# Second attention: the accumulated outputs copied out of PSUM by VectorE, not by ScalarE

## The chip, the cores and the metric

The kernel runs on one core of a Trainium2 chip: TensorE (PE) multiplies matrices into PSUM, ScalarE (ACT) and VectorE (DVE) work on PSUM and SBUF, GpSimd (POOL) on SBUF, and SyncE (SP) issues DMAs. Each engine takes its instructions in order, and engines wait for one another on semaphores. The metric is the device time of one execution in microseconds, lower is better.

## What is computed

Four sublayers follow each other on x of shape (8, 512, 128), each with a residual and a layer norm: an attention with softmax, a mixture of experts, a second attention with sigmoid weights, and a gated feed-forward. The change lies in the third. From the reference:

```python
def _L1_attn_ref(x, q_w, q_b, k_w, k_b, v_w, v_b, o_w, o_b, qn_scale, kn_scale):
    q = rms_norm(x, qn_scale) @ q_w.T + q_b
    k = rms_norm(x, kn_scale) @ k_w.T + k_b
    v = x @ v_w.T + v_b                      # 16 heads of 8
...
    q = apply_rotary(q, cos, sin)
    k = apply_rotary(k, cos, sin)
    scores = jnp.einsum('bhqd,bhkd->bhqk', q, k) * scale
    weights = jax.nn.sigmoid(scores)
    weights = weights / (jnp.sum(weights, axis=-1, keepdims=True) + EPS_RENORM)
    attn = jnp.einsum('bhqk,bhkd->bhqd', weights, v)
    attn = attn.transpose(0, 2, 1, 3).reshape(B, L, D)
    return attn @ o_w.T + o_b
...
x = _layernorm(x + _L1_attn_ref(x, ...))
```

## The kernel before

The second attention (`attention1`, from L1195) works batch by batch, 8 in all, b = 0 to 7. A batch is 32 steps, u = 0 to 31, and each engine has its own function `units` that says what it does at each step. The function `walk` (L270) calls it: batch 0 up to step 16, then a hardware loop over three pairs of batches, then the last one and a half batches unrolled. The order on each engine is thus fixed by the code, and the engines are held together by semaphores only.

At each step TensorE computes the scores of two heads against 128 keys (`s2`, L1321, into `ps_s[:, u % 2]`, two buffers), and ScalarE takes their sigmoid over 128x1024 elements into `prob` (L1275). Scores of step u wait for sigmoid u-2. At each odd step TensorE multiplies the probabilities of the two steps before with V (`pv`, L1333): product e stands at step 2e + 3, and sixteen of them make a batch. Eight products, for eight heads, accumulate in one PSUM bank, `ps_o`; then it must be copied to SBUF (`osb[:, n]`) before the next eight begin, since there is only one such bank. This copy is `take_o` (L1265), on ScalarE at the steps with u % 16 == 1, behind the sigmoid of that step: at step 17 for the first half of a batch (n = 0), at step 1 of the next batch for the second half (n = 1), and once after the last step. It counts up `o_taken`. Two users wait for that: product 8 (or 0 of the next batch) at step 19 or 3, and `turn_o` at step 20 or 4, where TensorE transposes `osb` into `ps_t`. The value also carries the sum of the weights, by which VectorE then divides (`divide`, L1463).

Other work is spread over the steps (constants at L66 to L71). For the finished batch, steps 4 to 15 hold the transposes, the projection with o_w, the residual and the norm. For a batch two ahead, VectorE starts `rms` at step 16 (L1415: copy of x, square, sum, scale; the four lines L1420 to L1427), POOL takes the power (L1548), VectorE multiplies x by it at step 19 (`scale_x`, L1431), and at steps 18, 20, 24 and 28 TensorE and VectorE do `front_use` and `take_front`: transposes of x and of the scaled x, and projections with rotary factors. V of the next batch is computed at step 2 (L1293) and taken by VectorE (L1458). The work for the batch two ahead exists for b = 0 to 5, V of the next batch in the loop for b = 1 to 6 at step 2. In the last batch VectorE also prepares feed-forward weights from step 18.

`osb` has two halves and is overwritten only after the transposes of one batch before (the wait on `ot_done`). After the block, `LastOutput` (L1577) goes on with the last half inside the feed-forward.

Of the kernel before, what the change touches and what calls it, by code (L numbers as in the profile page):

```python
# [12 lines left out]
ACT = mybir.ActivationFunctionType  # L13
# [3 lines left out]
NB = 8  # L17
T = 512
NT = T // P
# [5 lines left out]
PER_O = 2  # L25
NO = NG // PER_O
# [10 lines left out]
NE = NG * NT  # L37
# [84 lines left out]
def is_first(b):  # L122

    return isinstance(b, int) and b == 0


def is_last(b):

    return isinstance(b, int) and b == NB - 1
# [54 lines left out]
def v_tiles(flat):  # L184

    return flat[:, SLOT:].rearrange("p (k h c) -> p k h c", k=NT, h=H)
# [8 lines left out]
def output_parts(ps):  # L195

    return ps.rearrange("p (k j q c) -> p k j q c", k=NT, j=HG, q=PER_O)
# [8 lines left out]
def divide_outputs(nc, att, n, o, rec, done):  # L206

    to, spread = outputs_of(att, n), [P, NT, HG, HD]
    for q in range(PER_O):
        ins = nc.vector.tensor_tensor(to[:, :, :, q, :], o[:, :, :, q, 0:HD],  # L210
                                      rec[:, :, :, q].unsqueeze(3).broadcast_to(spread), ALU.mult)
    ins.then_inc(done, 1)
# [57 lines left out]
def walk(eng, units, loop_u=LOOP_U, lead=True):  # L270

    if lead:
        units(-1, 1, 0, NU, True, True, False, False)
    units(0, 0, 0, loop_u, False, True, True, False)
    with eng.Fori(0, (NB - 2) // 2) as i:
        for q in range(2):
            units(2 * i + q, q, loop_u, NU, True, True, True, False)
            units(2 * i + q + 1, 1 - q, 0, loop_u, False, True, True, True)  # L280
    units(NB - 2, 0, loop_u, NU, False, True, True, False)
    units(NB - 1, 1, 0, loop_u, False, False, True, True)
    units(NB - 1, 1, loop_u, NU, False, False, True, False)
# [911 lines left out]
def attention1(ctx, nc, g, c, e, xh, xl, ff):  # L1195
# [3 lines left out]
    with ExitStack() as inner:  # L1199
        def sb(name, shape, dt=F32):  # L1200
            return ctx.enter_context(nc.sbuf_tensor("a1_" + name, shape, dt))

        def sem(name):
            return ctx.enter_context(nc.semaphore("a1_" + name))
# [11 lines left out]
        osb = sb("osb", [P, 2, T])  # L1216
# [5 lines left out]
        ps_o = inner.enter_context(nc.psum_tensor("a1_ps_o", [P, T], F32))  # L1222
# [8 lines left out]
        s2_done, exp_done, pv_done = sem("s2_done"), sem("exp_done"), sem("pv_done")  # L1231
        o_taken, ot_done, rec_done, att_done, sum_done = (
            sem(n) for n in ("o_taken", "ot_done", "rec_done", "att_done", "sum_done"))


        S2_C, EXP_C, PV_C, O_C, OT_C, ATT_C = NU, 2, PSLOTS // 2, 1, 2, 1
# [4 lines left out]
        @block.sync  # L1241
        def _(sp):
            def step(b, p, qk_on, front):
                if front:

                    sp.wait_ge(s2_done, NU * b + S2_C)
                    load_stacks(sp, e, (qs[1 - p], ks[1 - p]), b + 1, 1 - p)
                if qk_on:
                    parts_to_dram(sp, e, b + 2, p)

            for src, ints, _, _ in ff["weights"]:
                sp.dma_start(ints[:, :, :], src).then_inc(ff["in"], 16)
            parts_to_dram(sp, e, 1, 1)
            with sp.Fori(0, (NB - 2) // 2) as i:
                step(2 * i, 0, True, True)
                step(2 * i + 1, 1, True, True)
            step(NB - 2, 0, False, True)

        @block.scalar
        def _(act):  # L1260
            def take(dst, src, ready, value, done):
                act.wait_ge(ready, value)
                nc.scalar.activation(dst, src, ACT.Copy).then_inc(done, 1)

            def take_o(b, n):  # L1265
                act.wait_ge(ot_done, NO * b + n - 1 + OT_C)
                take(osb[:, n, :], ps_o[:, :], pv_done, NE * b + PER_O * NT * (n + 1) + PV_C, o_taken)

            def units(b, p, u0, u1, qk_on, front, back, tail):
                for u in range(u0, u1):  # L1270
                    if back:
                        act.wait_ge(s2_done, NU * b + u + 1 + S2_C)
                        if u % 2 == 0:
                            act.wait_ge(pv_done, NE * b + u // 2 - PSLOTS // 2 + 1 + PV_C)
                        nc.scalar.activation(prob[:, u % PSLOTS, :, :], ps_s[:, u % 2, :, :], ACT.Sigmoid,  # L1275
                                             scale=float(HD) ** -0.5).then_inc(exp_done, 1)
                    if u % 16 == 1 and (back if u > 16 else tail):
                        take_o(*((b, u // 16 - 1) if u > 16 else (b - 1, NO - 1)))

            act.sem_inc(exp_done, EXP_C)  # L1280
            act.sem_inc(o_taken, O_C)
            walk(act, units, LOOP_U1, False)
            take_o(NB - 1, NO - 1)

        @block.tensor
        def _(pe):
# [122 lines left out]
        def _(dve):  # L1409
# [41 lines left out]
            def take_v(b, p):  # L1451

                if not isinstance(b, int) or b >= 2:
                    dve.wait_ge(pv_done, NE * (b - 1) + PV_C)
                if isinstance(b, int) and b < 2:
                    dve.wait_ge(cleared, 2 * b + 2)
                dve.wait_ge(v_done, b + 1)
                nc.vector.tensor_tensor(v_tiles(va[p])[:, :, :, 0:HD],  # L1458
                                        ps_f[:, 1, :].rearrange("p (k h d) -> p k h d", k=NT, h=H),
                                        vb[:, :].rearrange("p (h d) -> p h d", h=H).unsqueeze(1).broadcast_to(  # L1460
                                            [P, NT, H, HD]), ALU.add).then_inc(v_taken, 1)

            def divide(b, n):  # L1463

                o = output_parts(ps_t[:, :, :].rearrange("p k d -> p (k d)"))
                dve.wait_ge(ot_done, NO * b + n + 1 + OT_C)
                nc.vector.tensor_scalar_add(rec[:, :, :, :], o[:, :, :, :, HD], RENORM_EPS).then_inc(rec_done, 1)
                dve.wait_ge(rec_done, 2 * (NO * b + n) + 1)
                nc.vector.reciprocal(rec[:, :, :, :], rec[:, :, :, :]).then_inc(rec_done, 1)
                dve.wait_ge(rec_done, 2 * (NO * b + n) + 2)  # L1470
                divide_outputs(nc, att, n, o, rec, att_done)
# [30 lines left out]
            def units(b, p, u0, u1, qk_on, front, back, tail):  # L1502
                for u in range(u0, u1):
                    if is_first(b) and u == 0:
                        rms(1)
                    if is_first(b) and u == FIRST_AT[0] - 1:
                        scale_x(1)
                    if is_first(b) and u in FIRST_AT:
                        take_front(1, 1, FIRST_AT.index(u))
                    if front and u == (V_FIRST_AT if is_first(b) else V1_AT):  # L1510
                        take_v(b + 1, 1 - p)
                    if u % 16 == TURN_AT and (back if u > 16 else tail):
                        divide(*((b, u // 16 - 1) if u > 16 else (b - 1, NO - 1)))
                    if back and is_last(b) and u in FFN_W_AT:
                        if u == FFN_W_AT[0]:
                            dve.wait_ge(ff["in"], 16 * len(ff["weights"]))
                            dve.wait_ge(rope_done, 2 * NB + R_C)
                        prepare_ffn_weights(nc, dve, ff, turned[:, 0, 0:HID].rearrange("p (n d) -> p n d", n=NH3),
                                            u - FFN_W_AT[0])
                    if u == ALL_AT and tail:  # L1520
                        take_all(b - 1)
                    if u == PROJECT_AT and tail:
                        add_x(b - 1)
                    if u == NORM1_AT and tail:
                        norm(b - 1)
                    if u == X_AT and tail:
                        part_x(b - 1)
                    if u == RMS_AT and qk_on:
                        rms(b + 2)
                    if u == SCALE_AT and qk_on:  # L1530
                        scale_x(b + 2)
                    if u in FRONT_AT and qk_on:
                        take_front(b + 2, p, FRONT_AT.index(u))

            layernorm_stats(nc, dve, e["ln"], NB - 1, e["y"])
            take_v(0, 0)
            walk(dve, units, LOOP_U1, False)

        @block.gpsimd
        def _(pool):  # L1540
# [935 lines left out]
```

## Time and profile before

| | us |
|---|---|
| median of 3 runs | 1075.75 |
| lowest, highest | 1074.6, 1077.48 |
| the profiled execution | 1074.96 |
| its span, first to last instruction | 1073.2 |
| TensorE busy in the span | 1003.9 (94%) |
| VectorE | 814.2 (76%) |
| ScalarE | 735.5 (69%) |
| POOL | 459.8 (43%) |

The second attention's steps lie between about 722 and 1007 us of the span. Busy shares are of the whole span and mix stages with different limits; the table says little about this one. TensorE's rows come twice, PE for the matrix products and PEld for the loading of weights, which overlaps them; an idle time and its releaser stand in the row of the instruction that waited. Rows of one activation may overlap the next by their ends.

### The profile page before, as it was taken

To read this page: it belongs to the slowest core of one execution; us is meant where nothing else is said; L and a number is where in the kernel's file an instruction comes from. 1 tells how busy PE (TensorE), PEld (TensorE's weight loads), DVE (VectorE), ACT (ScalarE), POOL (GpSimd) and SP (SyncE) were. 2 spreads that over 40 slices of the span, in tenths; PEclk is the share of its full clock that TensorE was granted. 3 is DMA by queue.
4 is the path that set the end of the run, shared out by engine and by line. 5 is a ranking of instruction groups with operands and counts; after the bars stand their busy time and mean duration, and the time that the engine had idled before them with its cause. 6 is when DMAs were issued, how large, how long until landed. Compare 5 with 4: busy or idle time off the path is not lost. (4 is left out here: it accounts for less than half of the span.)

```text
span 1073.2 us, 20047 instructions
## 1 busy us (share of the span) xinstructions
PE 1003.9 (94%) x5764; PEld 473.8 (44%) x5764; DVE 814.2 (76%) x1891; ACT 735.5 (69%) x952; POOL 459.8 (43%) x464
## 2 busy tenths in 40 slices
PE   3999999999999998999999999989999999999996
PEld 1122222222222234788888887763332323222485
DVE  4879999999999975987888789957456545632577
ACT  1057777777777776555555555557888898899754
POOL 0313314133142715676777677565331333220175
PEclk7579999999999999999999999999999999999999
DMA  7363122231222003244323422441512331230011
GB/s 194 111 213 106 55 76 85 70 104 55 75 85 60 2 2 105 94 123 141 113 93 130 139 103 87 139 149 62 167 56 74 117 111 58 66 117 2 1 30 49
DMA packets 74091, 97.00 MB, mean 90 GB/s; under 512 B 12716, under 2 KB 42284, under 8 KB 73644
## 3 DMA queue, kind: packets, MB, share of 16 engines
q1 hardware_dynamic: 73048, 95.17, 28.5%
q10 hardware_dynamic: 992, 1.21, 0.4%
q8 instruction: 25, 0.41, 0.2%
q14 instruction: 26, 0.21, 0.1%
HBM read 68.16 MB, written 27.79 MB: 89 GB/s over the span
## 5 line engine op out<-in xcount | busy, mean ns | idle before, releaser
L688 DVE TENSOR_REDUCE a_nmax<-a_ps_f 128x1 f32<-128x512 f32 x512 | 320.1, 684 | 27.4 <-PE a_ps_f L543 26.3
L471 ACT ACTIVATE a_prob<-a_ps_s 128x1024 f32<-128x1024 f32 x256 | 251.2, 1022 | 74.8 <-PE a_ps_s L608 73.5
L1275 ACT ACTIVATE a_prob<-a_ps_s 128x1024 f32<-128x1024 f32 x256 | 244.9, 1030 | 35.6 <-PE a_ps_s L1329 34.8
L2102 POOL TENSOR_TENSOR moe_hl<-moe_hid,moe_hh 128x512 fp32r<-128x512 f32 x135 | 175.5, 1305 | 90.0 <-ACT moe_hh L1987 89.9
L543 PE MATMUL a_ps_f<-a_ks,a_qs 48*128 48x512 bf16 x512 | 176.9, 414 | 24.1 <-DMA a_ks<-parts_k 10.4
L1977 ACT ACTIVATE moe_ps<-moe_ps 128x512 f32<-128x512 f32 x128 | 74.5, 582 | 112.1 <-PE moe_ps L1904 111.5
L621 PE MATMUL a_ps_o<-a_prob,a_va 128*32 128x512 f32 x1024 | 138.1, 612 | 0.5 <-ACT a_prob L471 0.4
L1342 PE MATMUL a_ps_o<-a_prob,a_va 128*32 128x512 f32 x1024 | 137.2, 608 | 1.0 <-ACT a_prob L1275 0.5
L543 PEld LDWEIGHTS a_ps_f<-a_ks,a_qs 48*128 48x128 bf16 x512 | 40.7, 94 | 218.9 <-DVE a_nmax L688 188.3
L608 PE MATMUL a_ps_s<-a_qs,a_ks 51*128 51x512 bf16 x512 | 135.0, 388 | 1.7 <-ACT a_prob L471 1.5
L2028 DVE TENSOR_TENSOR moe_prod<-moe_cw,moe_ps 128x512 f32<-128x512 f32 x128 | 87.4, 683 | 29.3 <-PE moe_ps L1904 28.6
L1329 PE MATMUL a_ps_s<-a_qs,a_ks 48*128 48x512 bf16 x512 | 92.8, 388 | 12.3 <-ACT a_prob L1275 8.9
L2037 DVE TENSOR_TENSOR moe_hid<-moe_prod,moe_ps 128x512 f32<-128x512 f32 x128 | 87.0, 680 | 6.9 <-DVE moe_prod L2028 1.9
L259 POOL TENSOR_TENSOR a_parts<-a_qk,g_zero 128x512 bf16<-128x512 f32 x28 | 29.3, 1046 | 138.1 <-ACT a_qk L443 66.1
L1987 ACT ACTIVATE moe_hh<-moe_hid 128x512 fp32r<-128x512 f32 x136 | 84.6, 623 | 3.9 <-DVE moe_hid L2037 3.7
L1329 PEld LDWEIGHTS a_ps_s<-a_qs,a_ks 48*128 48x128 bf16 x512 | 23.6, 93 | 132.9 <-ACT a_prob L1275 106.0
L750 POOL TENSOR_TENSOR a_msplit<-a_nmax,g_zero 128x32 bf16<-128x32 f32 x16 | 3.8, 240 | 146.5 <-DVE a_nmax L688 146.5
L1902 PE MATMUL moe_ps<-moe_xh,moe_whig 128*128 (+1 forms) x136 | 54.8, 403 | 2.1 <-DVE moe_hid L2037 2.1
L1927 PE MATMUL moe_ps<-moe_hl,moe_whid 128*128 128x512 f32 x136 | 53.9, 396 | 1.4 <-POOL moe_hl L2102 1.4
L1902 PE MATMUL moe_ps<-moe_xh,moe_whiu 128*128 (+1 forms) x136 | 53.8, 395 | 0.0
L1922 PE MATMUL moe_ps<-moe_hh,moe_wlod 128*128 128x512 f32 x136 | 53.8, 395 | 0.0
L1903 PE MATMUL moe_ps<-moe_xh,moe_wlog 128*128 (+1 forms) x136 | 53.6, 394 | 0.0
(297 smaller groups left out, 1588.0 us busy)
## 6 DMA issues: line engine op xcount, KB each, us to landing
moe_cw<-r_weights SPq DMA_DIRECT2D x256, 128.0 KB, 2.9
parts_q<-a_parts SPq DMA_DIRECT2D x48, 256.0 KB, 2.5
a_qs<-parts_q SPq DMA_DIRECT2D x128, 96.0 KB, 2.4
parts_k<-a_parts SPq DMA_DIRECT2D x46, 256.0 KB, 2.5
a_ks<-parts_k SPq DMA_DIRECT2D x121, 96.0 KB, 2.4
a_xt<-in_x_t SPq DMA_DIRECT2D x8, 256.0 KB, 2.9
out_x<-g_X SPq DMA_DIRECT2D x7, 256.0 KB, 2.3
moe_wg<-in_wg SPq DMA_DIRECT2D x1, 1088.0 KB, 6.7
```

What stands on the lines that cost most here:

```text
L471: nc.scalar.activation(prob[:, u % PSLOTS, :, :], ps_s[:, u % 2, :, :], ACT.Exp, scale=float(P) ** -0.5).then_inc(exp_done, 1)
L543: nc.tensor.matmul(ps_f[:, bank, :], stack_rows(qs[p], h, QKR)[:, qt * P:(qt + 1) * P], stack_rows(ks[p], h, QKR), start=True, stop=True). ...
L608: mm = nc.tensor.matmul(ps_s[:, u % 2, i, :], stack_rows(ks[p], h, MXR)[:, kt * P:(kt + 1) * P], stack_rows(qs[p], h, MXR), start=True, st ...
L621: mm = nc.tensor.matmul(ps_o[j * CT:(j + 1) * CT, :], v_of_head(va[p], kt, grp * HG + j), prob[:, (2 * e + j // UN) % PSLOTS, j % UN, :], ...
L688: nc.vector.tensor_reduce(nmax[:, half_no, h % 2, col:col + 1], ps_f[:, bank, :], AX.X, ALU.max, negate=True).then_inc(max_done, 1)
L1275: nc.scalar.activation(prob[:, u % PSLOTS, :, :], ps_s[:, u % 2, :, :], ACT.Sigmoid, scale=float(HD) ** -0.5).then_inc(exp_done, 1)
L1329: mm = nc.tensor.matmul(ps_s[:, u % 2, i, :], stack_rows(ks[p], h, QKR)[:, kt * P:(kt + 1) * P], stack_rows(qs[p], h, QKR), start=True, st ...
L1342: mm = nc.tensor.matmul(ps_o[j * CT:(j + 1) * CT, :], v_of_head(va[p], kt, grp * HG + j), prob[:, (2 * e + j // UN) % PSLOTS, j % UN, :], ...
L1902: nc.tensor.matmul(dst, w[0][:, j, :], hi, start=True, stop=False)
L2028: nc.vector.tensor_tensor(prod[:, bank(j), :], cw[:, slot(j), :], ps_u[:, bank(j), :], ALU.mult).then_inc(prod_done, 1)
L2037: nc.vector.tensor_tensor(hid[:, hid_at(j), :], prod[:, bank(j), :], ps_g[:, bank(j), :], ALU.mult).then_inc(hid_done, 1)
L2102: nc.gpsimd.tensor_tensor(hl[:, part_at(j), :], hid[:, hid_at(j), :], hh[:, part_at(j), :], ALU.subtract).then_inc(hl_done, 1)
```

## The change

`take_o` goes from ScalarE's program to VectorE's. It stands there at the same steps, u % 16 == 1, ahead of `divide` and behind `take_v`, with the same waits and the same semaphore, as a `tensor_copy` in place of an activation with the function Copy. The last copy follows VectorE's walk. Nothing else is changed.

```diff
         @block.scalar
         def _(act):
-            def take(dst, src, ready, value, done):
-                act.wait_ge(ready, value)
-                nc.scalar.activation(dst, src, ACT.Copy).then_inc(done, 1)
-
-            def take_o(b, n):
-                act.wait_ge(ot_done, NO * b + n - 1 + OT_C)
-                take(osb[:, n, :], ps_o[:, :], pv_done, NE * b + PER_O * NT * (n + 1) + PV_C, o_taken)
-
             def units(b, p, u0, u1, qk_on, front, back, tail):
...
-                    if u % 16 == 1 and (back if u > 16 else tail):
-                        take_o(*((b, u // 16 - 1) if u > 16 else (b - 1, NO - 1)))
...
             walk(act, units, LOOP_U1, False)
-            take_o(NB - 1, NO - 1)
...
+            def take_o(b, n):
+                dve.wait_ge(ot_done, NO * b + n - 1 + OT_C)
+                dve.wait_ge(pv_done, NE * b + PER_O * NT * (n + 1) + PV_C)
+                nc.vector.tensor_copy(osb[:, n, :], ps_o[:, :]).then_inc(o_taken, 1)
+
             def divide(b, n):
...
                     if front and u == (V_FIRST_AT if is_first(b) else V1_AT):
                         take_v(b + 1, 1 - p)
+                    if u % 16 == 1 and (back if u > 16 else tail):
+                        take_o(*((b, u // 16 - 1) if u > 16 else (b - 1, NO - 1)))
                     if u % 16 == TURN_AT and (back if u > 16 else tail):
                         divide(*((b, u // 16 - 1) if u > 16 else (b - 1, NO - 1)))
...
             walk(dve, units, LOOP_U1, False)
+            take_o(NB - 1, NO - 1)
```

The place at step 17 on VectorE, in the loop. The names are those of the code (`a_` for the tiles of the attentions); REGISTER_ALU and ISA rows compute or wait for the value of a semaphore. Before:

```order
L1425 TENSOR_REDUCE a_ms<-a_xr 128x4 [waits a1_x_step]
L1426 REGISTER_ALU
L1427 TENSOR_SCALAR a_ms<-a_ms 128x4 [waits a1_x_step]
L1437 COPY a_xt<-a_ps_f 128x512 [waits a1_f_done]
L1430 REGISTER_ALU
L1431 TENSOR_TENSOR a_xr<-a_xb,a_rr 128x512 [waits a1_x_pow]
```

And now (lines of VectorE's program are 11 smaller up to `take_o`, since eight lines of ScalarE's are gone and three elsewhere):

```order
L1414 TENSOR_REDUCE a_ms<-a_xr 128x4 [waits a1_x_step]
L1415 REGISTER_ALU
L1416 TENSOR_SCALAR a_ms<-a_ms 128x4 [waits a1_x_step]
L1453 ISA
L1454 REGISTER_ALU [waits a1_ot_done]
L1455 COPY a_osb<-a_ps_o 128x512 [waits a1_pv_done]
L1426 COPY a_xt<-a_ps_f 128x512 [waits a1_f_done]
L1419 REGISTER_ALU
L1420 TENSOR_TENSOR a_xr<-a_xb,a_rr 128x512 [waits a1_x_pow]
```

The copy of `ps_o` stands between the last instruction of `rms` and the copy of the transposed x, with two more instructions on registers ahead of it, and the scaling of x (x_pow) is behind it.

The same place on ScalarE before:

```order
L1272 REGISTER_ALU
L1275 ACTIVATE a_prob<-a_ps_s 128x1024 [waits a1_s2_done]
L1266 ISA
L1262 REGISTER_ALU [waits a1_ot_done]
L1263 ACTIVATE a_osb<-a_ps_o 128x512 [waits a1_pv_done]
L1272 REGISTER_ALU
L1275 ACTIVATE a_prob<-a_ps_s 128x1024 [waits a1_pv_done,a1_s2_done]
```

And now:

```order
L1267 ACTIVATE a_prob<-a_ps_s 128x1024 [waits a1_s2_done]
L1264 REGISTER_ALU
L1266 REGISTER_ALU [waits a1_s2_done]
L1267 ACTIVATE a_prob<-a_ps_s 128x1024 [waits a1_pv_done]
L1264 REGISTER_ALU
```

The row of the copy and the two ahead of it are gone, and sigmoid follows sigmoid.

## Rows read from the trace of the kernel before

**Rows 1.** Stretch; busy of PE, PEld, DVE, ACT, POOL; TensorE clock; DMA share, GB/s

```profile
742.00:1006.00 264.00, 247.78 (x1752) 76.84 (x1744) 131.57 (x322) 236.05 (x256) 74.54 (x73) 1.00 0.27 84
```

**Rows 2.** Groups of instructions, 715 to 1010 us: busy us, mean ns | idle before

```profile
L1275 ACT ACTIVATE a_prob<-a_ps_s 128x1024 f32<-128x1024 f32 x256 | 244.9, 1030 | 35.6 <-PE a_ps_s L1329 34.8
...
L1342 PEld LDWEIGHTS a_ps_o<-a_prob,a_va 128*32 128x32 f32 x1024 | 20.2, 108 | 34.7 <-issue 28.5 <-ACT a_prob L1275 3.0 <-ACT a_osb L1263 2.3
```

**Rows 3.** The same view: copies out of PSUM on ScalarE and VectorE

```profile
L1263 ACT ACTIVATE a_osb<-a_ps_o 128x512 f32<-128x512 f32 x16 | 9.8, 612 | 1.2 <-PE a_ps_o L1342 1.2
...
L1475 DVE COPY a_att_t<-a_ps_t 128x512 f32<-128x512 f32 x7 | 4.8, 692 | 7.9 <-PE a_ps_t L1362 7.9
```

**Rows 4.** Timeline, place A: start us, us, engine, line, operation [idle <-releaser]

```profile
781.59 0.60 ACT L1263 ACTIVATE a_osb<-a_ps_o 128x512 f32<-128x512 f32 x1
...
782.06 0.69 DVE L1425 TENSOR_REDUCE a_ms<-a_xr 128x4 f32<-128x512 f32 x1
...
782.07 2.88 ACT L1275 ACTIVATE a_prob<-a_ps_s 128x1024 f32<-128x1024 f32 x3
...
782.26 0.16 PEld L1342 LDWEIGHTS a_ps_o<-a_prob,a_va 128*32 128x32 f32 x8 [0.23 <-ACT a_osb L1263]
...
782.78 0.17 DVE L1427 TENSOR_SCALAR a_ms<-a_ms 128x4 f32<-128x4 f32 x1
...
782.86 0.68 DVE L1437 COPY a_xt<-a_ps_f 128x512 f32<-128x512 f32 x1
...
783.26 0.10 PEld L1329 LDWEIGHTS a_ps_s<-a_qs,a_ks 48*128 48x128 bf16 x2 [0.84 <-ACT a_prob L1275]
...
783.58 0.42 PEld L1355 LDWEIGHTS a_ps_t<-g_ident,a_osb 128*128 128x128 f32 x4 [0.23 <-issue]
...
784.07 0.69 DVE L1431 TENSOR_TENSOR a_xr<-a_xb,a_rr 128x512 f32<-128x512 f32 x1 [0.53 <-POOL a_rr L1548]
...
784.81 0.42 PEld L1312 LDWEIGHTS a_ps_f<-g_ident,a_xr 128*128 128x128 f32 x4 [0.82 <-DVE a_xr L1431]
...
785.40 0.10 PEld L1329 LDWEIGHTS a_ps_s<-a_qs,a_ks 48*128 48x128 bf16 x2 [0.17 <-issue]
...
785.84 1.02 ACT L1275 ACTIVATE a_prob<-a_ps_s 128x1024 f32<-128x1024 f32 x1 [0.89 <-PE a_ps_s L1329]
...
924.25 0.60 ACT L1263 ACTIVATE a_osb<-a_ps_o 128x512 f32<-128x512 f32 x1
```

**Rows 5.** Timeline, VectorE, a waiting register instruction between two operations

```profile
771.80 0.69 DVE L1479 TENSOR_TENSOR a_att<-a_ps_t,a_ob 128x512 f32<-128x512 f32 x1 [2.04 <-PE a_ps_t L1369]
...
772.63 0.69 DVE L1482 TENSOR_TENSOR a_att<-a_att,g_X 128x512 f32<-128x512 f32 x1
```

**Rows 6.** Timeline, place B, start of batch 2

```profile
799.11 0.63 ACT L1263 ACTIVATE a_osb<-a_ps_o 128x512 f32<-128x512 f32 x1
...
800.05 0.69 DVE L1458 TENSOR_TENSOR a_va<-a_ps_f,a_vb 128x512 f32<-128x512 f32 x1 [2.86 <-PE a_ps_f L1295]
...
800.39 3.77 ACT L1275 ACTIVATE a_prob<-a_ps_s 128x1024 f32<-128x1024 f32 x4 [0.65 <-PE a_ps_s L1329]
...
800.41 0.16 PEld L1342 LDWEIGHTS a_ps_o<-a_prob,a_va 128*32 128x32 f32 x8 [0.42 <-issue]
```

**Rows 7.** Timeline, place A of batch 0, and place D

```profile
749.16 0.42 PEld L1312 LDWEIGHTS a_ps_f<-g_ident,a_xr 128*128 128x128 f32 x4 [1.77 <-DVE a_xr L1431]
...
1007.57 0.60 ACT L1263 ACTIVATE a_osb<-a_ps_o 128x512 f32<-128x512 f32 x1 [1.25 <-PE a_ps_o L1342]
```

**Rows 8.** Timeline, place C, step 17 of batch 7

```profile
991.17 0.69 DVE L1500 TENSOR_TENSOR ff_xl<-a_ps_t,ff_xh 128x512 fp32r<-128x512 f32 x1
...
992.76 0.10 PEld L1329 LDWEIGHTS a_ps_s<-a_qs,a_ks 48*128 48x128 bf16 x2 [0.80 <-ACT a_prob L1275]
...
993.25 0.16 PEld L1342 LDWEIGHTS a_ps_o<-a_prob,a_va 128*32 128x32 f32 x8 [0.39 <-ACT a_osb L1263]
...
995.26 0.19 DVE L1467 TENSOR_SCALAR a_rec<-a_ps_t 128x32 f32<-128x32 f32 x1 [2.74 <-PE a_ps_t L1355]
```

## The prediction, made before the result was known

> **What bounds the kernel now.** The stretch to read is the second attention. The row that groups it [rows 1] shows TensorE busy 247.78 of 264 us, ScalarE 236.05, VectorE 131.57, at a granted clock of 1.00 (2.4 GHz). So TensorE and ScalarE are both nearly full, and VectorE is half empty. That share doesn't say which of the two full engines a shorter ScalarE queue would help; the gaps do. The groups of instructions [rows 2] give the two sides of one chain: the sigmoids (L1275, 256 of them) wait 34.8 us for scores from TensorE, and the products with V (L1342) wait 2.3 us for the ScalarE copy. ScalarE alternates with TensorE: scores have two buffers, so a score step u waits for the sigmoid of u-2 and the sigmoid of u for the scores of u. Where ScalarE runs without a gap, it sets the pace; where TensorE also has projections or transposes to do, TensorE does. Next the prices of the copy [rows 3], then each kind of place where one stands, in the timeline [rows 4 to 8].
>
> **Sixteen places, four kinds.** A copy stands behind step 1 and step 17 of each batch, and one after the last step. By the timeline they are: A, step 17 of batches 0 to 5, where VectorE has the RMS work of a later batch queued ahead of it (6 places, of which batch 0 is special); B, step 1 of batches 1 to 6, where TensorE computes V of the next batch (6); C, step 17 of batch 6 and steps 1 and 17 of batch 7, with none of that (3); D, the last one (1).
>
> **Place A, batches 1 to 5 (five places, from 781.59 to 924.25, so 35.67 us apart, one batch).** Before, the ScalarE copy starts at 781.59 and the next sigmoid at 782.07, so the copy takes 0.48 us of ScalarE's queue; its row says 0.60 because ends overlap. It ends at 782.19 and TensorE's first V product of the new group starts at 782.26, 0.07 later [rows 4]. That product can't start earlier than o_taken. Afterwards the copy is VectorE's, in order behind L1427, which starts at 782.78 because it ends the chain copy, square, sum, scale of the RMS work. The next VectorE instruction starts at 782.86 today, with no register instruction between; the new copy has two ahead of it, one with a wait (the order above shows them). What these cost isn't shown in isolation. The nearest rows: L1482 follows L1479 by 0.83, or 0.14 after its end, with one such waiting instruction between [rows 5], whereas L1427 follows the end of L1425 by 0.03 [rows 4]. So one costs about 0.10; from below nothing, if they are fetched while L1427 runs; from above 0.18 for two. A gain is excluded, since they stand ahead of the copy. I take 0.09: copy from 782.95, and 0.69 long, by L1475, the same form out of PSUM on VectorE [rows 3]. It ends at 783.64, and the product starts at 783.71 instead of 782.26, 1.45 later.
>
> Not all of this reaches the end. Behind the product stand scores 20 (1.00 later, by 782.26 to 783.26), the transposes of the output (0.32 more), then transposes of the scaled input, which today stand idle until 784.81, "0.82 <-DVE a_xr", then scores 21 at 785.40, 0.59 further [rows 4]. With the late product these come at 784.71, 785.03, 785.62 (transposes of this form take 0.59) and 786.21. Is the scaled input ready at 785.62? VectorE now runs copy until 783.64, L1437 (0.68) until 784.35, and L1431 (0.69) until 785.07, as POOL's power is ready by 784.07: yes, with 0.5 to spare. So the late product costs 786.21 - 785.40 = 0.81 us; 0.64 of its 1.45 is swallowed by a wait that existed. ScalarE's sigmoid after scores 21 starts 0.44 behind them, with an idle gap of 0.89 ahead of it [rows 4]: it waits for TensorE, so the 0.48 us that the removed copy frees only makes that gap longer. Sigmoid 21 and all behind it start 0.81 later. Register instructions at nothing or 0.18 give 0.72 to 0.90. From there both engines run in lockstep, POOL and DMA work hangs on the same steps, and I find no wait later in the batch for something that didn't move. Five times: +4.05 us.
>
> **Place A, batch 0.** There TensorE stands at the scaled input until 749.16, for 1.77 us [rows 7]. That wait is behind the V product and longer than the 1.45 us by which the product could be late, so it hides all of it: 0, and 0.1 if it leaks.
>
> **Place B.** The copy on ScalarE starts at 799.11, yet ScalarE then still idles 0.65 us, until 800.39, for scores that TensorE starts only after V [rows 6]. Without the copy that gap grows to 1.1 us and nothing starts earlier. VectorE is idle for 2.86 us before L1458 at 800.05 [rows 6]; a 0.69 us copy there is over by about 799.7, ahead of the V product at 800.41 that needs it. Six times 0; from above 0.1 each if POOL's work beside it slows the copy.
>
> **Place C.** Here the copy delays something: the V product at 993.25 stands 0.39 "<-ACT a_osb", whereas scores 19 were issued at 992.76, and 0.32 behind them it could go, at 993.08 [rows 8]. VectorE finished its transposed input at 991.86 and has only weight preparation for much later; its copy ends near 992.7. So TensorE goes 0.17 earlier. ScalarE's sigmoids start 0.48 earlier at first, but the one that needs scores 22 comes 0.17 earlier only. Three times -0.17: -0.51 us. The weight work is pushed 0.7 us, under VectorE's later idle time of 2.74 us [rows 8].
>
> **Place D.** The last V product ends, ScalarE copies from 1007.57 and the next part of the program begins behind that [rows 7]. VectorE, idle there, takes 0.69 for 0.61 [rows 3]: +0.08 us.
>
> **A rule against the change.** The copy rows say 691 ns on VectorE against 612 on ScalarE [rows 3], 0.08 us. By the Trainium skill, "Advanced Engine Details and Errata", The Read-Write Bubble, "ScalarE is closer to PSUM, VectorE is closer to SBUF - use accordingly". Rule and rows agree on the sign, but duration alone would make at most 16 times 0.08, 1.3 us; what the queue ahead of the copy adds is not in that rule, and it is the larger part here.
>
> **Sum.** +4.05 + 0 + 0 - 0.51 + 0.08 = +3.6 us. The profiled execution took 1074.96 us (1.76 more than its span, and 0.8 under the median of 1075.75), so 1078.6 on its own scale and 1079.4 on the median's. With the register cost at either end, +3.2 to +4.1.
>
> **Rivals.** First, faster, because ScalarE is the bound. 16 times 0.48 is 7.7 us, which gives 1068.1. For it: ScalarE is at 236 of 264 us and VectorE at 132 [rows 1]. Against: in A and B ScalarE is idle right behind the copy [rows 4, 6]. [...] 0.08.
>
> Second, no measurable change: the 0.81 is made good later in each batch. It decides if behind scores 21 TensorE has slack against ScalarE again before ScalarE's lateness counts, as ScalarE has had its copy taken out. For: TensorE waits for sigmoids often in the stretch. Against: sigmoid 21 itself waits for scores. Then only -0.51 + 0.08 is left, about 1075.3. 0.15.
>
> Third, slower by more: the cover under the late product is gone. The 0.64 counted as hidden rests on the scaled input being ready at 785.62. If L1437 and L1431, pushed behind the new copy, finish over 0.55 later than I reckon (by POOL's port traffic or register instructions), the input is itself late. Then the whole 1.45 goes through: 5 x 1.45 = 7.25, less 0.43, about 1082.5. For: VectorE is in order and takes two 128x512 operations ahead of L1431. Against: the 0.5 of room. 0.10.
>
> **Numbers.** Forecast 0.67, rivals 0.08, 0.15 and 0.10. About 0.3% (3.2 us) is what a measurement can tell from no change, and the line is at 1079.0, near my forecast: I give three quarters of the forecast's chance to slower and one quarter to no change. Slower: 0.50 + 0.10 = 0.60. No change: 0.17 + 0.13 = 0.30. Faster: 0.10, with a little from the second rival. The forecast's own range is 1078.5 to 1080.5. The range reaches over rivals two and three, 1074.8 to 1082.6, and leaves out the first.
>
> **What would show each step.** In the profile of after: at place A the copy on VectorE right behind the scale instruction of the RMS work, TensorE idle some 1.4 us for it ("<-DVE a_osb"), and the wait for a_xr gone or small; the batch period 36.5 in place of 35.67 us in the loop. At B no idle time on the copy, and 1.1 us of ScalarE idle behind it. At C the product 0.2 us earlier. Wrong would be: a period of 35.67 or less, or a wait for a_xr that persists next to that for a_osb.

## The result, and the profile after

| | before | after |
|---|---|---|
| median of 5 runs | 1077.34 us | 1083.57 us |
| lowest, highest | 1074.6, 1079.11 | 1082.69, 1086.66 |
| ratio, 95% interval | | 1.0065 [1.0047, 1.0084] |
| profiled execution | 1074.96 | 1086.66 |
| its second attention, from the sigmoid of step 12 of batch 0 to the last one, start to start | 267.1 | 274.7 |

The change makes the kernel 6.2 us slower. The forecast had the side right, +3.6 us, and the size wrong by a factor of 1.7. The time lies 1.0 us above the range of 1074.8 to 1082.6. Part of that is not the change: the range was built on a median before of 1075.75 us (3 runs), which is 1077.34 with 5. As a difference, +6.2 us would still be inside the range, far from the forecast. In a second measurement (c1_changed, below) the ratio was 1.0045 [1.0024, 1.0066].

The profiled execution after is the slowest of its five, and 4.1 us of its 11.7 lie ahead of the second attention, whose first sigmoid starts at 726.9 and not at 722.8. The program up to there is the same in both kernels, and in the other profiles below this start lies anywhere between 721.9 and 725.6. So I compare stretches of the second attention, not whole spans. They begin at step 12 of batch 0, because TensorE also idles for 1.7 us where this attention begins, and around there the granted clock falls in 11 of the 14 profiles and stays at 1.00 in three; that moves the first steps by up to 1.1 us whatever the kernel. The row of the kernel before has a mean of 0.79 there:

```profile
716.00:732.00 16.00, 12.52 (x64) 5.48 (x67) 7.94 (x19) 8.07 (x10) 9.22 (x13) 0.79 0.12 37
```

Place A first, in the timeline of the kernel after, batch 1; it answers to [rows 4]. Columns: start us, us, engine, line, operation, idle before and releaser. VectorE's copy is now L1455, the V product L1331, the sigmoid L1267, the scaled input L1420.

```profile
788.21 0.17 DVE L1416 TENSOR_SCALAR a_ms<-a_ms 128x4 f32<-128x4 f32 x1
788.41 0.69 DVE L1455 COPY a_osb<-a_ps_o 128x512 f32<-128x512 f32 x1
...
789.15 0.16 PEld L1331 LDWEIGHTS a_ps_o<-a_prob,a_va 128*32 128x32 f32 x8 [1.69 <-DVE a_osb L1455]
...
789.61 0.68 DVE L1420 TENSOR_TENSOR a_xr<-a_xb,a_rr 128x512 f32<-128x512 f32 x1
790.15 0.10 PEld L1318 LDWEIGHTS a_ps_s<-a_qs,a_ks 48*128 48x128 bf16 x2 [0.84 <-issue]
...
790.47 0.42 PEld L1344 LDWEIGHTS a_ps_t<-g_ident,a_osb 128*128 128x128 f32 x4 [0.23 <-issue]
...
790.86 0.47 PEld L1301 LDWEIGHTS a_ps_f<-g_ident,a_xr 128*128 128x128 f32 x4
...
791.49 0.10 PEld L1318 LDWEIGHTS a_ps_s<-a_qs,a_ks 48*128 48x128 bf16 x2 [0.17 <-issue]
```

The copy starts 0.20 us behind the start of the last RMS instruction, and TensorE stands until it is done before it can begin the product (1.69 us in the row of the weight load, 1.40 in that of the product itself). The wait for the scaled input, 0.82 us in [rows 4], is gone: its row has no idle time. That is the chain of the forecast, step for step.

Now the same line in the five batches. These are all the copies at step 17 of batches 1 to 5, from VectorE's timeline.

```profile
788.41 0.69 DVE L1455 COPY a_osb<-a_ps_o 128x512 f32<-128x512 f32 x1
...
824.78 0.69 DVE L1455 COPY a_osb<-a_ps_o 128x512 f32<-128x512 f32 x1
...
862.69 0.69 DVE L1455 COPY a_osb<-a_ps_o 128x512 f32<-128x512 f32 x1
...
900.58 0.69 DVE L1455 COPY a_osb<-a_ps_o 128x512 f32<-128x512 f32 x1
...
936.91 0.69 DVE L1455 COPY a_osb<-a_ps_o 128x512 f32<-128x512 f32 x1
```

The batches take 36.37, 37.91, 37.89 and 36.33 us; before, all took 35.65 to 35.68. So there are two lengths: some 0.67 more than before, and 1.57 on top of that in some. Where the 1.57 lies is seen at batch 2, in the stretches of 2 us around its copy (busy time and count of PE, PEld, DVE, ACT, POOL; then the granted TensorE clock, DMA share, GB/s):

```profile
822.00:824.00 2.00, 1.85 (x16) 0.61 (x8) 1.91 (x4) 2.00 (x3) 0.00 (x0) 1.00 0.07 27
824.00:826.00 2.00, 0.59 (x6) 0.16 (x8) 1.93 (x5) 1.29 (x2) 1.01 (x1) 0.97 0.00 0
826.00:828.00 2.00, 2.00 (x12) 0.49 (x5) 0.67 (x2) 0.19 (x1) 0.00 (x0) 0.50 0.00 0
828.00:830.00 2.00, 2.00 (x14) 1.44 (x16) 1.16 (x5) 0.96 (x2) 0.00 (x0) 0.67 0.00 0
830.00:832.00 2.00, 2.00 (x20) 0.35 (x12) 1.17 (x2) 1.63 (x2) 0.00 (x0) 1.00 0.00 0
```

and in the timeline there:

```profile
825.52 1.63 PE L1331 MATMUL a_ps_o<-a_prob,a_va 128*32 128x512 f32 x8 [1.41 <-DVE a_osb L1455]
...
827.08 0.61 PE L1318 MATMUL a_ps_s<-a_qs,a_ks 48*128 48x512 bf16 x2
```

TensorE idles 1.41 us for the copy, and then its granted clock is at 0.50, 1.2 in place of 2.4 GHz, for about 3.4 us by the three rows. The eight parts of the product take 1.63 us, against 1.06 in batch 1. The row of the whole stretch before, [rows 1], has the clock at 1.00 throughout. In the execution after it falls three times between 742 and 1010 us: near 754 (batch 0), 826 and 864, each time directly behind a place where TensorE idled for 1.4 us.

### The profile page after: what moved, and what is told of

Its sections match the earlier page's. It is cut to its first block and busy times, and to the rows that moved or that the text cites. A ratio compares the mean times of both kernels' runs of the same rounds, so it can differ in the third digit from the quotient of the medians.

```text
span 1084.8 us, 20041 instructions
## 1 busy us (share of the span) xinstructions
PE 1009.2 (93%) x5764; PEld 477.3 (44%) x5764; DVE 824.9 (76%) x1907; ACT 729.9 (67%) x936; POOL 459.6 (42%) x464
## 5 line engine op out<-in xcount | busy, mean ns | idle before, releaser
L1267 ACT ACTIVATE a_prob<-a_ps_s 128x1024 f32<-128x1024 f32 x256 | 245.2, 1029 | 48.7 <-PE a_ps_s L1318 48.0
L543 PE MATMUL a_ps_f<-a_ks,a_qs 48*128 48x512 bf16 x512 | 176.4, 413 | 23.8 <-DMA a_ks<-parts_k 10.1
L1331 PE MATMUL a_ps_o<-a_prob,a_va 128*32 128x512 f32 x1024 | 139.1, 616 | 7.8 <-DVE a_osb L1455 7.2
```

The lines of the kernel that those rows point to most:

```text
L543: nc.tensor.matmul(ps_f[:, bank, :], stack_rows(qs[p], h, QKR)[:, qt * P:(qt + 1) * P], stack_rows(ks[p], h, QKR), start=True, stop=True). ...
L1331: mm = nc.tensor.matmul(ps_o[j * CT:(j + 1) * CT, :], v_of_head(va[p], kt, grp * HG + j), prob[:, (2 * e + j // UN) % PSLOTS, j % UN, :], ...
```

## The experiments

Each kernel but c2_changed and c3_filled, which have one profiled run each, was timed beside the kernel before on the same chip. The column "batch" is the distance between scaled inputs (L1431 before) of batches 1 to 5 without a fall of the clock; "stretch" goes from the sigmoid of step 12 of batch 0 to the last one; "falls" are those of the granted clock in that stretch. Batch, stretch and falls are of the one profiled run.

| kernel | median us (before) | ratio, 95% | batch us | stretch us | falls |
|---|---|---|---|---|---|
| before | | | 35.66 | 267.1 | 0 |
| after | 1083.57 (1077.34) | 1.0065 [1.0047, 1.0084] | 36.34 | 274.7 | 3 |
| c1_changed, the same | 1082.81 (1078.07) | 1.0045 [1.0024, 1.0066] | 36.34 | 273.2 | 2 |
| c2_changed, the same | 1078.86, one run | | 36.33 | 270.0 | 0 |
| e1_second_half | 1077.37 (1077.44) | 1.0004 [0.9987, 1.0021] | 35.66 | 267.0 | 0 |
| e2_first_half | 1082.65 (1077.44) | 1.0062 [1.0042, 1.0082] | 36.33 | 271.6 | 1 |
| e3_filled | 1079.6 (1077.44) | 1.0017 [0.9997, 1.0037] | 36.33 | 270.0 | 0 |
| c3_filled, the same | 1077.96, one run | | 36.33 | 270.0 | 0 |
| e4_inside_rms | 1080.48 (1077.44) | 1.003 [1.001, 1.005] | 36.14 | 270.7 | 1 |
| e5_before_late_front | 1066.01 (1076.43) | 0.9911 [0.9886, 0.9936] | 34.37 | 258.3 | 0 |
| e6_after_late_front | 1076.08 (1076.43) | 1.001 [0.9991, 1.0029] | 35.83 | 265.4 | 0 |
| e7_inside_late_front | 1067.83 (1076.43) | 0.9927 [0.9901, 0.9952] | 34.37 | 258.1 | 0 |
| e8_inside_front21 | 1078.47 (1076.43) | 1.0015 [0.9997, 1.0034] | 36.19 | 269.3 | 0 |
| c4_before_front21 | 1079.75 (1078.07) | 1.0017 [1.0006, 1.0027] | 36.19 | 269.6 | 0 |

### Which copies cost: e1_second_half and e2_first_half

e1 leaves the copies at step 17 on ScalarE and moves the others; e2 is the reverse. VectorE's side of e1:

```diff
-                    if u % 16 == 1 and (back if u > 16 else tail):
+                    if u == 1 and tail:
                         take_o(*((b, u // 16 - 1) if u > 16 else (b - 1, NO - 1)))
```

> One part of the change alone: VectorE takes only the copies at step 1 and the last one (places B, one of the three places C, and D), ScalarE keeps those at step 17. Theory: all of the loss comes from step 17 of batches 0 to 5, where the VectorE copy stands behind the RMS work. Then this kernel is as fast as before: 0 for B, -0.17 for step 1 of batch 7, +0.1 for the last, so within 1 us of before, and no wait of TensorE of over 0.5 us for the copy. Rival (each VectorE copy costs its longer duration or disturbs POOL): 8 of 16 copies moved, so about half of the loss, +3 us.

> The other part alone: VectorE takes only the copies at step 17 (places A and two of C), ScalarE keeps those at step 1. Theory: the whole loss is here. 5 x 0.69 for the late product, 2 x -0.17, so +3.1 us by queueing alone, and with a fall of the TensorE clock behind the 1.4 us gap at two or three of the six places A at 1.5 us each, +6 to +7.5. Rival (the loss is spread over the copies): +3 us, half of the change's.

e1 is as fast as before, e2 as slow as the whole change, though its 5.2 us is less than the 6 to 7.5 expected, and its profile has one fall and not two or three. The times alone leave the eight copies at step 1 and at the end a cost or gain of about 2 us; the profile of e1 narrows that, with a batch of 35.66 us and a stretch of 267.0. The loss is at step 17. At place B the timeline of the kernel after shows why, as [rows 6] did: VectorE's copy runs while TensorE computes V, and ScalarE's idle time behind it went from 0.65 to 1.14 us.

```profile
842.85 0.97 PEld L1284 LDWEIGHTS a_ps_f<-a_w,a_xt 128*128 128x128 f32 x8 [0.84 <-issue]
...
842.99 0.69 DVE L1455 COPY a_osb<-a_ps_o 128x512 f32<-128x512 f32 x1 [2.01 <-PE a_ps_o L1331]
...
844.45 4.85 ACT L1267 ACTIVATE a_prob<-a_ps_s 128x1024 f32<-128x1024 f32 x5 [1.14 <-PE a_ps_s L1318]
```

### The clock: e3_filled, and more profiles

Ten transposes of the identity into `ps_t`, never read, ahead of the product that waits:

```diff
+            def fill_in(b):
+                pe.wait_ge(x_parted, b + XP_C)
+                for k in range(FILL):
+                    nc.tensor.transpose(ps_t[:, k % NT, :], ident[:, :], ident[:, :])
...
+                    if u == 19 and qk_on:
+                        fill_in(b)
                     if u % 2 == 1 and (back if u > 1 else tail):
                         pv(*((b, p, u // 2 - 1) if u > 1 else (b - 1, 1 - p, NE - 1)))
```

> The changed kernel, with ten transposes of the identity added on TensorE at step 19 of batches 0 to 5, ahead of the product that waits for the VectorE copy; their result is never read. They keep TensorE busy in the idle time before that product and delay nothing, as they end (about 1.1 us) before the copy does (1.4 us). Theory: the 3 us that my sum lacks are the TensorE clock, which falls to half behind the idle gap. With the gap filled the clock stays at 1.00 through the second attention and the time is +3.0 us against before (only 5 x 0.69 - 0.51 + 0.08), although more work is done: 3 us faster than the changed kernel. Rival (the extra time is queueing or noise, not the clock): the same as the changed kernel, +6 to +7, or more by the added work.

The timeline of e3_filled, batch 1, shows that the filling does not delay the product, which still starts 0.74 us behind the start of the copy, as in the kernel after.

```profile
785.07 1.31 PE L1352 MATMUL a_ps_t<-g_ident 128*128 128x128 f32 x10
...
785.79 0.69 DVE L1464 COPY a_osb<-a_ps_o 128x512 f32<-128x512 f32 x1
...
786.54 1.06 PE L1332 MATMUL a_ps_o<-a_prob,a_va 128*32 128x512 f32 x8 [0.15 <-DVE a_osb L1464]
```

and the second attention's inner stretch there, then of the kernel after, has these granted clocks:

```profile
744.00:1010.00 266.00, 253.36 (x1806) 83.47 (x1805) 141.96 (x338) 228.12 (x239) 75.52 (x73) 1.00 0.27 83
```

```profile
744.00:1010.00 266.00, 246.60 (x1716) 78.15 (x1716) 140.85 (x335) 223.79 (x235) 76.58 (x74) 0.98 0.27 83
```

With more work on TensorE the kernel is 3.05 us faster than e2_first_half of the same comparison (1079.6 against 1082.65), and 2.2 us slower than before; 3.0 had been expected. e2 moves only the copies at step 17, e3 all of them, but e1 shows that the others make no such difference. All of e3's batches take 36.33 us.

> The changed kernel once more, for a second profile and more times. Theory: a batch without a fall of the TensorE clock takes 36.3 us (0.67 more than before), one with a fall 37.9; the falls stand behind the idle gap at place A and come in some of the six places; time +5 to +7. Rival: the falls seen in the first profile were chance and come at other places as well, or not again.

> The changed kernel, a third profile: the same as for c1_changed. Falls of the clock only behind the gap at place A.

> The kernel of e3_filled again (ten transposes whose result is never read, ahead of the late product): a second profile. Theory: no fall of the clock at places A of batches 1 to 5, and batches of 36.33 us. Rival: falls come here too.

The changed kernel's second profile has two falls, near 821 and 858 us, at place A of batches 2 and 3; the third has none, and its run took 1078.86 us. The median of c1 is 4.7 us over the kernel before, just under the 5 to 7 expected. These are the same windows in c1_changed and then in c2_changed, whose places A lie within about 1 us of those of c1:

```profile
820.00:825.00 5.00, 4.63 (x24) 2.08 (x28) 2.91 (x8) 1.45 (x3) 0.67 (x1) 0.66 0.00 0
857.00:862.00 5.00, 3.75 (x18) 1.66 (x18) 2.53 (x7) 2.09 (x3) 1.01 (x1) 0.66 0.00 0
```

```profile
820.00:825.00 5.00, 4.13 (x32) 1.55 (x32) 3.99 (x10) 2.69 (x3) 1.01 (x1) 1.00 0.00 0
857.00:862.00 5.00, 4.81 (x40) 1.71 (x40) 3.65 (x9) 2.69 (x4) 0.50 (x1) 1.00 0.00 0
```

The stretch's lengths add up: 270.0 us with no fall, 273.2 with two, 274.7 with three; 1.57 each gives 273.1 and 274.7. Over the five profiles with the gap of 1.4 us at place A (after, c1, c2, e2, e6) the clock fell at 5 of the 25 places of batches 1 to 5; over the two with the gap filled, at 0 of 10, and in the kernel before at none. These counts alone are thin.

The mean granted clock of every single run says more. From it follows how long the clock was at its lower level in that run: twice the span times the missing share. About half of the runs, of most kernels, have one low stretch of some 58 us in their first 70 us; I take that off. What is left includes, in every kernel, a few us at the end of the span and whatever falls stand elsewhere. On average, uncertain by 1 to 2 us:

| kernel | runs | us at the lower clock | kernel before, beside it |
|---|---|---|---|
| e1_second_half | 10 | 15.1 | 13.1 (31 runs) |
| e2_first_half | 10 | 22.4 | 13.1 |
| e3_filled | 10 | 12.6 | 13.1 |
| c1_changed | 6 | 20.5 | 15.4 (14 runs) |
| after | 5 | 24.0 | not on record |

At 3.4 us a fall, e2 has 2.7 more falls a run than the kernel before, and c1 1.5 more. With the gap filled (e3) there are none more. The means don't say where in the program the falls are; the profiles do that. So the fall behind the unfilled gap is shown by e2 against e3. With 1.57 us a fall and some 3 us of queueing, c1 should by this estimate be 5.5 us over the kernel before and e2 7.2; their medians are 4.7 and 5.2 over it, their means 4.9 and 6.3. So the estimate is somewhat high; 1.57 us is the price of a fall at place A, and what one costs elsewhere may differ.

### Where the copy stands on VectorE: e4_inside_rms

```diff
                 nc.vector.tensor_copy(xb[:, :, :], X[:, b, :, :]).then_inc(x_step, 1)
+                if take is not None:
+                    take_o(*take)
                 dve.wait_ge(x_step, c + 1)
...
-                        rms(b + 2)
+                        rms(b + 2, (b, 0))
```

> The changed kernel with the VectorE copy at step 17 of batches 0 to 5 moved up, between the copy of x and its square in the RMS work. By before's times VectorE can take it at 781.33 (the sums are complete by 780.9), so the product is no longer late. But square, sum, scale, POOL's power and the scaled input all come 0.72 later. Theory (VectorE's chain and the V product compete for the same 0.7 us): the wait only moves to the transposes of the scaled input, which come 0.7 late, so again +3 us by queueing, with a gap of about 1.5 us ahead of them and some falls of the clock: +3 to +7. Rival (only the late product matters): this placing removes the loss, within 1 us of before or faster.

1.003, a batch of 36.14 us. The wait did move: in its timeline, batch 1, the product is on time and the transposes wait for the scaled input.

```profile
782.85 0.16 PEld L1331 LDWEIGHTS a_ps_o<-a_prob,a_va 128*32 128x32 f32 x8 [0.23 <-issue]
...
785.13 0.69 DVE L1422 TENSOR_TENSOR a_xr<-a_xb,a_rr 128x512 f32<-128x512 f32 x1 [0.53 <-POOL a_rr L1547]
...
785.88 0.42 PEld L1301 LDWEIGHTS a_ps_f<-g_ident,a_xr 128*128 128x128 f32 x4 [1.29 <-DVE a_xr L1422]
```

So the rival that only the late product mattered falls. At steps 17 to 20 VectorE's chain is on TensorE's path: 0.7 us put into it comes out as 0.48 us of each batch inside the RMS work, and as 0.67 behind it. Its one fall is at place A of batch 0, behind a gap of 1.84 us; behind its five gaps of 1.05 us there is none.

### The cover taken away: e5, e6 and e7

```diff
-FRONT_AT = (18, 20, 24, 28)
+FRONT_AT = (18, 22, 26, 30)
```

> The kernel before (copies on ScalarE), with the front work for the batch two ahead spread later: its transposes and projections stand at steps 18, 22, 26 and 30 in place of 18, 20, 24 and 28. The transposes of the scaled input, for which TensorE stood 0.82 us (1.77 in batch 0) at step 20, then find it ready. Theory: that wait is the cover under which the late product hid, and it is itself a loss: 5 x 0.6 + 1.5, so up to -4.5 us, -2 to -4.5 against before, as later steps may give some back. Rival (the wait is given back in the later steps, which are then fuller): within 1 us of before, or slower.

> The changed kernel with the same later front steps (18, 22, 26, 30). This takes away the cover from under the late product. Theory: against e5_before_late_front the product's whole lateness of 1.4 us counts in batches 1 to 5 and 0.5 in batch 0, so +7 us or more, plus falls of the clock behind the gap, less 0.5 of place C: e5 + 6.5 to + 9. Rival (the lateness is no loss of its own; only the chain over the scaled input was): e5 + 0 to + 2.

> All copies on VectorE, the one at step 17 inside the RMS work behind the copy of x (as in e4), and the front steps later (as in e5). Theory: now neither the product nor the scaled input is waited for, so VectorE's 0.7 us costs nothing, and ScalarE is rid of 0.48 us per copy where it sets the pace: e5 - 3 to e5 + 0, and the fastest of all, 1070 to 1075. Rival (VectorE copies cost something wherever they stand): slower than e5 by 2 us or more.

e6 against e5 has no cover over the late product, as in the third rival of the prediction, though for another reason: there the scaled input would have been late, here its step was moved. A batch takes 35.83 against 34.37 us, 1.46 more, where 1.45 was the product's lateness. The cover was worth the rest: with it the same lateness costs 0.67. These are two scaled inputs of e5, then of e6:

```profile
814.77 0.69 DVE L1431 TENSOR_TENSOR a_xr<-a_xb,a_rr 128x512 f32<-128x512 f32 x1 [0.53 <-POOL a_rr L1548]
...
849.13 0.69 DVE L1431 TENSOR_TENSOR a_xr<-a_xb,a_rr 128x512 f32<-128x512 f32 x1 [0.53 <-POOL a_rr L1548]
```

```profile
819.23 0.68 DVE L1420 TENSOR_TENSOR a_xr<-a_xb,a_rr 128x512 f32<-128x512 f32 x1
...
855.05 0.68 DVE L1420 TENSOR_TENSOR a_xr<-a_xb,a_rr 128x512 f32<-128x512 f32 x1
```

The times are 10.1 us apart, more than the 6.5 to 9 expected. The stretch accounts for about 7; and e6's runs are at the lower clock for 14.0 us on average, e5's four for 7.5.

e5 itself gained 10.4 us, over twice what I had expected at most. I had counted only TensorE's wait, 0.6 us a batch, but a batch is 1.29 shorter. Before, ScalarE idles behind that wait twice, 0.89 us ahead of sigmoid 21 and then 0.37 ahead of sigmoid 22. In e5's timeline six sigmoids, of steps 18 to 23, follow one another without a gap, and the next waits 0.29:

```profile
778.38 5.86 ACT L1275 ACTIVATE a_prob<-a_ps_s 128x1024 f32<-128x1024 f32 x6
...
782.11 0.66 PE L1312 MATMUL a_ps_f<-g_ident,a_xr 128*128 128x128 f32 x4
...
784.53 2.85 ACT L1275 ACTIVATE a_prob<-a_ps_s 128x1024 f32<-128x1024 f32 x3 [0.29 <-PE a_ps_s L1329]
```

Counted from sigmoid 16 of the same batch, sigmoid 22 starts 1.24 us earlier in e5 than before, in batches 1 to 3 alike, and 1.29 is reached two steps into the next batch. So nearly all of the gain is those two idle times of ScalarE; the later projections shift its waits about and add 0.05. Batch 0, with the longer wait of [rows 7], gains 2.24 us, and five times 1.29 more make the 8.7 us by which the stretch is shorter. The rest of the 10.4 goes with the clock: e5's runs are at the lower level for 7.5 us on average, those of the kernel before beside them for 13.2.

In e7, with all copies on VectorE and neither wait left, a batch takes 34.37 us, exactly e5's. So VectorE's copy costs nothing where its chain has two steps to spare. It also gains nothing in a batch, though ScalarE is rid of 0.48 us at each copy: e7 had been expected to be the fastest and at 1070 to 1075 us, and it measures 1067.83, 1.8 us over e5, with overlapping intervals. Its stretch is 0.3 us shorter than e5's; its runs are at the lower clock for 13.1 us on average, e5's for 7.5. That answers the first rival of the prediction once more: ScalarE's copies were not what a batch waited for.

### Which step: e8_inside_front21 and c4_before_front21

e8 is e7 with front steps 18, 21, 25 and 29; c4 has these steps with the copies on ScalarE.

> As e7, with the front steps at 18, 21, 25 and 29. One step is 1.1 us, and the scaled input comes about 0.7 later than before; with the 0.6 that TensorE stood already, it is late by 1.3 us at step 20, so by 0.2 or so at step 21. Theory: nearly all of e7's gain against e4, within 1.5 us of e7. Rival (what helps e7 is the spreading of the projections and not the scaled input's lateness): half way between e4 and e7.

> The kernel before with the front steps at 18, 21, 25 and 29. Odd steps hold scores and V product, even ones scores only. Theory: front work on odd steps stands on top of a V product and starves ScalarE, whoever makes the copies; then this is as slow as e8_inside_front21, +1 to +3 against before, 10 us slower than e5_before_late_front with 18, 22, 26, 30. Rival (only the scaled input's lateness at step 21 cost e8 its gain): here it is 0.7 us earlier, so as fast as e5, -10.

e8's expectation, within 1.5 us of e7, was wrong by 9 us: it is 10.6 us slower than e7, with 36.19 us a batch. c4 settles what of: without any copy on VectorE, and the scaled input 0.7 us earlier, it takes 36.19 too. So it isn't the copy or the scaled input, it is the odd steps. How an odd step costs is my reading of one timeline and was not tested by itself. In the timeline of e8 the transposes follow a V product within the same step, and the sigmoid behind them waits:

```profile
783.07 1.07 PE L1331 MATMUL a_ps_o<-a_prob,a_va 128*32 128x512 f32 x8
...
784.07 0.66 PE L1301 MATMUL a_ps_f<-g_ident,a_xr 128*128 128x128 f32 x4
...
785.16 3.77 ACT L1267 ACTIVATE a_prob<-a_ps_s 128x1024 f32<-128x1024 f32 x4 [0.87 <-PE a_ps_s L1318]
```

Product and transposes together are 1.7 us (783.07 to 784.73) without scores, and ScalarE has two score buffers, 1.9 us of sigmoids, of which one is mostly used up by then.

The best of all these is e5_before_late_front: the copies left on ScalarE and the front steps later, 0.9% under the kernel before.

## Why the prediction was wrong, point by point

- **Place A, mechanism: right.** The product is late by the copy behind the RMS chain, part of it hides under the old wait for the scaled input, and nothing later gives it back. e1 and e2 place the loss, e6 prices the whole lateness (1.46, forecast 1.45).
- **Place A, size: 0.67 and not 0.81 us.** The register instructions cost what was assumed: the copy starts 0.20 behind the RMS instruction (forecast 0.17). The term that was off is the chain behind: I let the transposes of the scaled input come 0.59 after those of the output and scores 21 another 0.59 later, 1.18 in all. Measured are 0.39 (790.47 to 790.86) and 0.63, 1.02 in all. 5 x 0.67 is 3.35 for 4.05.
- **Place A, batch 0: nothing,** as forecast. In c1_changed and c2_changed no sigmoid up to the next place A is later than before. (The scaled input of batch 1 is 0.12 later, as VectorE's chain is longer there, but nothing waits for it.)
- **Place B: 0,** as forecast; e1 shows it, and in c2_changed no sigmoid behind these copies shifts.
- **Place C: right in sign, too large.** The product at step 17 of batch 7 now starts 0.32 behind scores 19 without a wait (the rows below), as the forecast had it. The sigmoids behind the three places come 0.17, 0.05 and 0.16 us earlier in c2_changed, where 0.17 each was forecast: the place at step 1 of batch 7 gains little, and in e1 too it is 0.05.

```profile
1004.48 0.10 PEld L1318 LDWEIGHTS a_ps_s<-a_qs,a_ks 48*128 48x128 bf16 x2 [0.80 <-ACT a_prob L1267]
...
1004.80 0.16 PEld L1331 LDWEIGHTS a_ps_o<-a_prob,a_va 128*32 128x32 f32 x8 [0.23 <-issue]
```

- **Place D: +0.12 us,** forecast 0.08. From the last V product to the transposes that use its copy it is 2.10 us before (the rows below) and 2.22 in the kernel after (1017.94 to 1020.16).

```profile
1006.38 1.06 PE L1342 MATMUL a_ps_o<-a_prob,a_va 128*32 128x512 f32 x8 [0.52 <-ACT a_prob L1275]
1008.48 0.63 PE L1595 MATMUL ff_ps<-g_ident,a_osb 128*128 128x128 f32 x4 [1.03 <-PEq L1199]
```

- **The sum: 3.1 us of queueing** (3.35 + 0 + 0 - 0.38 + 0.12), forecast 3.6. Kernels without a fall of the clock in the stretch show it: c2_changed, c3_filled and e3_filled have 270.0 us for 267.1 before, to which place D comes on top. The times of e3_filled, +2.2 us with an interval of -0.3 to +4.0, agree.
- **The missing term: the clock.** The step that failed stands in the first sentences of the prediction: it read a granted clock of 1.00 in [rows 1] and then took it as given for the kernel after, while the same text made a gap of 1.4 us on TensorE in every batch. So the sum put the clock at nothing. What the runs show in its place is 3 falls in the first profile, at 1.57 us each, which is half the size of all the queueing, and on average 1.5 more falls a run in c1 and 2.7 in e2 than in the kernel before. With the gap filled, in e3, they are gone. The range reached over 1082.5 only for another mechanism, the third rival, which did not happen here: the cover held. That the measured difference would still fit the range is luck.
- **The rule against the change** (the Trainium skill, "Advanced Engine Details and Errata", The Read-Write Bubble): the copy is 0.69 us on VectorE against 0.60 on ScalarE in these traces as well, yet where eight such copies move (e1) a batch stays at 35.66 us. The difference in duration counts only at place D, 0.12 us, where everything waits for the copy.

The Trainium skill, "TensorE: Matmul & The Clock Gate", HAM oscillation — how this bites in real kernels, has the fall of the clock behind long idle gaps of TensorE as its rule. Traces here agree that it falls behind idle time, but gaps of 1.4 us, shorter than those the rule warns of, were enough in 5 cases of 25; the measurement decides. The Trainium skill, "Perfetto Trace Analysis", Matmul Optimizations, asks for matmuls back to back. e3_filled agrees: with the 1.4 us gap filled there is no fall in 10 places.

## What to carry to other kernels

Before work moves to an engine with a low busy share, look at what that engine does at the very step where the work will stand, and who waits for it there: VectorE was half empty, and still its queue was full for 2 us at the step that mattered. When a change makes a new gap on TensorE, count the chance of a clock fall in addition to the gap, and check it against a version with the gap filled by useless matmuls. Compare the mean granted clock of all runs, not only the profiles. And read a wait that a change hides under as a loss of its own: here moving the step that waited and the two behind it by two steps was worth 10 us, more than the question that was asked. By one step it was worth nothing.

## What the hardware showed unexpectedly

- A gap of 1.4 us in an otherwise busy TensorE was followed by a fall of the granted clock to 0.50 in 5 of 25 cases, for about 3.4 us, and cost 1.57 us each time. The same kernel shows 0, 2 or 3 falls in this stretch in different executions. The five gaps of 1.05 us in e4_inside_rms, and those of 0.58 us at the same place in the kernel before, were followed by none.
- Adding ten transposes whose result is thrown away at each of six places made the kernel about 3 us faster than its nearest like in the same comparison (e3 against e2). The time at the lower clock went from 22.4 to 12.6 us a run.
- In the kernel before, batch 0 has a gap of 1.54 us on TensorE (its weight load waits 1.77, [rows 7]) with no fall; in the kernel after, the same place, with 1.45 us, had one, and in c1 and c2, also with 1.45, none. The gap makes a fall possible, not certain; what decides between them isn't shown.
